# One stage for keys, values and queries: values made transposed, pieces turned by transposing DMAs

## The chip, the cores and the metric

The kernel runs on one core of a Trainium2 chip. The metric is the device time of one execution in microseconds; the median of three runs of the kernel before is 1968.65 us (1966.84 to 1968.81).

## What is computed

Two layers over x (8 x 256 tokens = 2048, 512 wide) and a context of the same size. The changed part is the first half of the second layer, cross attention with 16 heads of 32 columns, where queries and keys are quantised per row and head, values per column over all tokens:

```python
q = (x @ Wq + bq).reshape(1, B * N, H, hd)
kv = (cond @ Wkv + bkv).reshape(1, -1, 2, H, hd)
k, v = (kv[:, :, 0], kv[:, :, 1])
q = jnp.transpose(q * scale, (0, 2, 1, 3))
k = jnp.transpose(k, (0, 2, 1, 3))
v = jnp.transpose(v, (0, 2, 1, 3))
q = _fq_sym(q, axis=-1)      # s = max|q| / 127; round(q / s) * s
k = _fq_sym(k, axis=-1)
v = _fq_sym(v, axis=2)       # one scale per head and column
attn = jnp.einsum('bhqd,bhkd->bhqk', q, k)
attn = jax.nn.softmax(attn.astype(jnp.float32), axis=-1)
attn = _fq_unsigned(attn, axis=-1)
out = jnp.einsum('bhqk,bhkd->bhqd', attn, v)
```

Here x is normalised per row first, and cond is the context. Around it stand a first attention, a gated network of 4-bit weights, the projection and a ternary network.

## The kernel before

The stages follow one another in `build` (L117), each a block of its own: `mix_rows`, `gated_ffn`, `keys_values`, `queries`, `attend`, `project`, `ternary_ffn`. A block starts when all engines have left the one before. P is 128, NT = 16 tiles of 128 tokens, CH = 4 chunks of 128 columns.

`keys_values` (L1049) loops over 16 tiles of tokens. SyncE fetches a tile of the transposed context (`cT`, 256 KB, two buffers, L1101). TensorE makes the keys (`psK`, L1207) and the values (`psV`, L1213), each four f32 products of 128x128 by 512 columns, which the trace shows as eight instructions, and then turns the previous tile's key pieces by 16 transposes of 128x128 bf16 (`psT`, L1220). VectorE adds both biases (L1149, L1152), takes each head's maximum (L1155), quantises the keys (L1156 to L1160) and splits them into three bf16 parts, high, middle and low, of which the fourth quarter is zero (L1167 to L1169); ScalarE copies the high part (L1134), takes the values' sizes (L1130) and stores the turned pieces in `KT` (L1122). After the loop the values' scales are made from a running maximum by transposes and products with the identity (L1235, L1239), and VectorE and GpSimd scale all 16 tiles of values (L1115, L1195), which VectorE rounds into `V` (L1198).

`queries` (L1243) loads its weights (L1277), and per tile VectorE normalises x (L1290), TensorE transposes it (`psX`, L1352), ScalarE copies that (L1327), TensorE multiplies (`psQ`, L1359), VectorE adds the bias, quantises and writes three copies (L1297 to L1309), TensorE turns them by 16 transposes (L1366) and ScalarE stores them in `QO` (L1332).

The order on every engine is the order of the program; engines wait for one another by semaphores only. `attend` (L1387) reads `KT`, `QO` and `V`; its first product is at L1454. Its turned probabilities come from a transposing DMA (L1443), and `gated_ffn` uses the same kind for 128 x 2048 bf16 (L808).

## Time and profile before

| | us |
|---|---|
| median of three runs | 1968.65 |
| the profiled execution | 1971.55 |
| its span, first to last instruction | 1969.8 |
| TensorE busy in it | 1760.5 |
| VectorE busy | 1584.5 |
| ScalarE busy | 1230.8 |
| GpSimd busy | 918.7 |

The span is one execution on the hardware profiler's clock, from the first to the last instruction. Busy time counts an engine's own instructions; matmuls are pipelined, so the start of one and the start of the next tell the pace better than the durations. In the timeline a row is a run of like instructions: start, length, engine, line, operation, written tile, read tiles, shapes, count, and in brackets the idle time before it and what ended it. PEclk is TensorE's granted clock as a share of full speed.

### The profile page before, as it was taken

To read this page: it belongs to the slowest core of one execution; us is meant where nothing else is said; L and a number is where in the kernel's file an instruction comes from. 1 tells how busy PE (TensorE), PEld (TensorE's weight loads), DVE (VectorE), ACT (ScalarE), POOL (GpSimd) and SP (SyncE) were. 2 spreads that over 40 slices of the span, in tenths; PEclk is the share of its full clock that TensorE was granted. 3 is DMA by queue.
4 is the path that set the end of the run, shared out by engine and by line. 5 is a ranking of instruction groups with operands and counts; after the bars stand their busy time and mean duration, and the time that the engine had idled before them with its cause. 6 is when DMAs were issued, how large, how long until landed. Compare 5 with 4: busy or idle time off the path is not lost. (4 is left out here: it accounts for less than half of the span.)

```text
span 1969.8 us, 32510 instructions
## 1 busy us (share of the span) xinstructions
PE 1760.5 (89%) x11262; PEld 786.4 (40%) x11262; DVE 1584.5 (80%) x2930; ACT 1230.8 (62%) x2011; POOL 918.7 (47%) x935
## 2 busy tenths in 40 slices
PE   4999989599999969939899999999999969579998
PEld 1322322144444435425344444444444434234443
DVE  5899999776776678868899999999999956774433
ACT  4888876455454324414599999999999965222111
POOL 6576764464544300020188888888888850000000
PEclk8999999799999989959899999999999989799999
DMA  9764640300000021000054555555565553000000
GB/s 210 205 163 108 160 119 12 110 11 11 22 0 22 0 80 34 24 27 0 16 108 108 108 108 107 109 106 110 103 109 108 108 131 142 6 6 17 22 22 22
DMA packets 334720, 147.54 MB, mean 75 GB/s; under 512 B 290544, under 2 KB 306928, under 8 KB 333424
## 3 DMA queue, kind: packets, MB, share of 16 engines
q1 hardware_dynamic: 334576, 145.70, 31.8%
q8 instruction: 81, 1.33, 0.3%
q14 instruction: 63, 0.52, 0.1%
HBM read 70.15 MB, written 4.19 MB: 38 GB/s over the span
## 5 line engine op out<-in xcount | busy, mean ns | idle before, releaser
L1571 ACT ACTIVATE a_prob<-a_psS,a_bias,q_scale 128x1024 uint8<-128x1024 f32 x512 | 610.2, 1211 | 28.3 <-PE a_psS L1464 24.4
L1500 DVE TENSOR_REDUCE a_tops<-a_psM 128x1 f32<-128x512 f32 x1024 | 622.6, 677 | 2.2 <-PE a_psM L1454 0.8
L1550 POOL CAST a_wide<-a_pairs 128x2048 int16<-128x2048 uint8 x256 | 481.4, 1891 | 99.5 <-DMA a_pairs<-a_prob 84.8
L1454 PE MATMUL a_psM<-KT,QO 128*128 128x512 bf16 x1024 | 370.7, 387 | 5.6 <-PEq L1248 2.2
L1464 PE MATMUL a_psS<-KT,QO 128*128 128x512 bf16 x1024 | 305.4, 380 | 4.3 <-ACT a_prob L1571 4.3
L1476 PEld LDWEIGHTS a_psO<-V,a_wide 128*128 128x128 f16 x4096 | 175.1, 96 | 146.4 <-DVE QO L1513 23.0
L1476 PE MATMUL a_psO<-V,a_wide 128*128 128x32 bf16 x4096 | 181.5, 177 | 21.8 <-DVE QO L1513 15.6
L854 DVE SCALAR_TENSOR_TENSOR g_sum<-g_psG,gu_scale,g_sum 128x512 f32<-128x512 f32 x176 | 124.2, 745 | 89.7 <-PE g_psG L1006 74.9
L832 POOL TENSOR_TENSOR g_sum<-g_sum 128x512 f32<-128x512 f32 x88 | 126.3, 1436 | 140.4 <-DVE g_sum L854 140.4
L489 ACT ACTIVATE prob<-psT 128x512 f32<-128x512 f32 x256 | 142.9, 598 | 68.5 <-PE psT L698 68.1
L953 ACT ACTIVATE g_sum<-g_psG,gu_scale 128x512 f32<-128x512 f32 x176 | 111.2, 681 | 109.6 <-PE g_psG L1006 108.9
L554 DVE TENSOR_REDUCE rmax<-psS 128x1 f32<-128x512 f32 x256 | 158.6, 673 | 12.1 <-PE psS L684 10.5
L1019 PE MATMUL g_psY<-raw_dn,g_hT 128*128 128x512 f32 x352 | 163.1, 592 | 0.0
L1454 PEld LDWEIGHTS a_psM<-KT,QO 128*128 128x128 bf16 x1024 | 96.9, 96 | 137.4 <-DVE a_tops L1500 133.3
L1845 ACT ACTIVATE t_h<-t_psH,t_b 128x512 f32<-128x512 f32 x64 | 44.0, 687 | 162.3 <-PE t_psH L1869 143.5
L684 PE MATMUL psS<-ks,qs 128*128 128x512 f16 x256 | 93.1, 395 | 41.9 <-POOL qs L413 22.0
L1464 PEld LDWEIGHTS a_psS<-KT,QO 128*128 128x128 bf16 x1024 | 96.4, 98 | 68.7 <-ACT a_prob L1571 12.6
L413 POOL TENSOR_TENSOR qs<-xs,q_sub 128x512 f16<-128x512 f32 x64 | 74.8, 1191 | 87.6 <-ACT q_sub L481 83.3
L1571 ACT ACTIVATION_READ_ACCUMULATOR a_prob<-a_psS,a_bias,q_scale 128x1 f32 x512 | 105.5, 206 | 0.0
L1869 PE MATMUL t_psH<-t_xT_hi,t_w1q 128*128 128x512 f16 x256 | 98.4, 385 | 6.6 <-ACT t_h L1845 5.1
L1881 PE MATMUL t_psY<-t_w2q,t_hT_hi 128*128 128x512 f16 x256 | 99.1, 387 | 2.0 <-DVE t_hT_lo L1806 2.0
L694 PE MATMUL psT<-qs,ks 128*128 128x512 f16 x256 | 98.4, 384 | 0.9 <-ACT prob L489 0.9
(211 smaller groups left out, 2862.0 us busy)
## 6 DMA issues: line engine op xcount, KB each, us to landing
xs<-in_x SPq DMA_DIRECT2D x64, 256.0 KB, 6.5
cs<-in_ctx SPq DMA_DIRECT2D x64, 256.0 KB, 8.4
KT<-in_w SPq DMA_DIRECT2D x2, 4096.0 KB, 21.1
raw_gu<-in_gu SPq DMA_DIRECT2D x4, 1408.0 KB, 8.4
vs<-in_ctxT SPq DMA_DIRECT2D x16, 256.0 KB, 2.8
k_cT<-in_ctxT SPq DMA_DIRECT2D x16, 256.0 KB, 2.7
a_pairs<-a_prob SPq DMA_TRANSPOSE x256, 2.7
out<-x_sb SPq DMA_DIRECT2D x16, 256.0 KB, 2.0
```

What stands on the lines that cost most here:

```text
L489: act.activation(prob[:, g % RING, :], psT[g % NT3][:, :], ACT.Exp, scale=float(D0) ** -0.5).then_inc(exped, 1)
L554: v.reduce_max(rmax[j % 2][:, n:n + 1], psS[(NG * j + n) % 3][:, :], AX.X).then_inc(maxed, 1)
L832: pool.tensor_tensor(a[:, :], a[:, :], b[:, :], ALU.add).then_inc(totalled, 1)
L854: v.scalar_tensor_tensor(out=acc[:, :], in0=psG[q % CH][:, :], scalar=gu_scale[:, i * FG + p, g:g + 1], in1=acc[:, :], op0=ALU.mult, op1=A ...
L953: act.activation(part_sum[g][i][m % 3][:, :], psG[q % CH][:, :], ACT.Copy, scale=gu_scale[:, i * FG + p, g:g + 1]).then_inc(scaled, 1)
L1019: mm = pe.matmul(psY[k][:, :], hT[t % 2][:, f, k * P:(k + 1) * P], w_dn[:, f, :], start=(f == 0), stop=(f == FG - 1))
L1454: pe.matmul(psM[n % NM][:, :], QOf[:, i * P:(i + 1) * P], KTf[:, keys:keys + 512], start=True, stop=True).then_inc(shown, 1)
L1464: mm = pe.matmul(psS[g % NS][:, c * 512:(c + 1) * 512], QOf[:, i * P:(i + 1) * P], KTf[:, keys + c * 512:keys + (c + 1) * 512], start=True ...
L1476: mm = pe.matmul(psO[:, h * D1:(h + 1) * D1], wide[i % NV][:, parity, c, :].bitcast(F16), V[:, h, 2 * c + parity, :], start=(parity == 0 a ...
L1500: v.reduce_max(tops[i // JOIN % NB][:, i % JOIN, c:c + 1], psM[n % NM][:, :], AX.X).then_inc(topped, 1)
L1550: pool.tensor_copy(wide[i % NV][:, :, :, :].rearrange("p k c q -> p k (c q)"), both).then_inc(widened, 1)
L1571: act.activation(prob[i % NP][:, k * HK:(k + 1) * HK], psS[g % NS][:, :], ACT.Exp, scale=q_scale[:, i:i + 1], bias=bias[i // JOIN % NB][:, ...
```

## The change

`keys_values` and `queries` become one stage, `keys_values_queries`. The values are made transposed, 128 columns by 512 tokens in a unit, with the weights' columns as the stationary operand; ScalarE adds their bias while it empties the bank, and a unit of 128 columns over all 2048 tokens (four units) is quantised at once by VectorE. Products of values and keys alternate in the order of the list `ORDER` over four banks, `psA`, which the queries use too. The biases of keys and queries are added as one more product: rows of three bf16 parts, made by `bias_rows`, with ones. The high and middle parts of the keys are the upper half-words of f32 numbers, copied by ScalarE; VectorE makes the rest and the low part. The pieces of keys and queries and the quantised values are turned by transposing DMAs from SyncE (16 + 16 + 4, 512 KB each) in place of TensorE's transposes and ScalarE's copies. The loops are written out. The weights, the context and the values lie where `QO` will be written. `V` has its dimensions in another order, and tokens lie in it in another order to match the turned probabilities, which `KT`'s interleaving did before.

Removed lines are those of the two functions printed above; from the new function the core is shown.

```diff
@@ -115,7 +115,7 @@
 
 
 def build(nc, x_in, ctx_in, ctxT_in, gamma_in, gu_in, gus_in, dn_in, dns_in, wq_in, bq_in, wkv_in,
-          bkv_in, wp_in, bp_in, w1_in, b1_in, w2_in, b2_in, out):
+          bkv_in, bv_in, wp_in, bp_in, w1_in, b1_in, w2_in, b2_in, out):
     with ExitStack() as ctx:
         def sb(name, shape, dt):
             return ctx.enter_context(nc.sbuf_tensor(name, shape, dt))
@@ -154,12 +154,11 @@
             def asb(name, shape, dt):
                 return att.enter_context(nc.sbuf_tensor(name, shape, dt))
 
-            env["V"] = asb("V", [P, H1, NT, D1], BF16)
+            env["V"] = asb("V", [P, NT, H1, D1], BF16)
             env["v_scale"] = asb("v_scale", [P, CH], F32)
-            keys_values(env, ctxT_in, wkv_in, bkv_in)
             env["QO"] = asb("QO", [P, NT * H1, P], BF16)
             env["q_scale"] = asb("q_scale", [P, NT * H1], F32)
-            queries(env, wq_in, bq_in)
+            keys_values_queries(env, ctxT_in, wkv_in, bkv_in, bv_in, wq_in, bq_in)
             env["e_sum"] = asb("e_sum", [P, NT * H1 * 2], F32)
             attend(env)
             project(env, wp_in, bp_in, w1_in, w2_in)
@@ -1046,11 +1045,13 @@
                     down(*t_f_k)
 
 
-def keys_values(env, ctxT_in, wkv_in, bkv_in):
-
-
-
-    nc, KT, V, v_scale, id_f, id_b = (env[n] for n in ("nc", "KT", "V", "v_scale", "id_f", "id_b"))
+def keys_values_queries(env, ctxT_in, wkv_in, bkv_in, bv_in, wq_in, bq_in):
...
+    nc, x_sb, KT, V, v_scale, QO, q_scale, id_f, mv, rstd = (env[n] for n in (
+        "nc", "x_sb", "KT", "V", "v_scale", "QO", "q_scale", "id_f", "mv", "rstd"))
+    NA = 4
+    AHEAD = 4
+    NU = CH * NTC
     with ExitStack() as ctx:
         def sb(name, shape, dt):
             return ctx.enter_context(nc.sbuf_tensor(name, shape, dt))
@@ -1061,327 +1062,339 @@
...
+        words = flat(QO[:, :, :]).bitcast(F32)
+        wkv = words[:, 0:2 * CH * DM].rearrange("p (c n) -> p c n", c=CH)
+        vT = [words[:, 2 * CH * DM + i * TOK:2 * CH * DM + (i + 1) * TOK] for i in range(2)]
+        cT = words[:, 2 * CH * DM + 2 * TOK:].rearrange("p (c n) -> p c n", c=CH)
...
+        UNITS = [(2 * (u // 8) + u % 2, u % 8 // 2) for u in range(NU)]
+        ORDER = [("v", u) for u in range(AHEAD)]
+        for i in range(NU - AHEAD):
+            ORDER += [("k", i), ("v", AHEAD + i)]
+        ORDER += [("k", t) for t in range(NU - AHEAD, NT)] + [("q", t) for t in range(NT)]
+        SLOT = {item: s for s, item in enumerate(ORDER)}
...
+        def high_half(ap):
...
+            return ap.bitcast(BF16).rearrange("p (h d k) -> p h d k", d=D1, k=2)[:, :, :, 1]
...
+        def free(eng, g):
...
+            if g >= 2:
+                eng.wait_ge(turned[g % 2], 16 * (g // 2))
...
+            def turn_values(c):
+                sp.wait_ge(v_ready, c + 1)
+                out = V[:, :, c * HT:(c + 1) * HT, :].rearrange("p t h d -> p t (h d)").bitcast(I16)
+                sp.dma_start_transpose(out, vq[:, :].bitcast(I16)).then_inc(v_turned, 16)
...
+            def turn_keys(t):
+                sp.wait_ge(high_ready, 2 * t + 2)
+                sp.wait_ge(lo_ready, t + 1)
+                sp.dma_start_transpose(KT[:, :, t * P:(t + 1) * P].bitcast(I16),
+                                       parts[t % 2][:, :, :, :].rearrange("p h k d -> p (h k d)").bitcast(I16)
+                                       ).then_inc(turned[t % 2], 16)
...
+            sp.dma_start(bv[:, :], bv_in).then_inc(loaded[0], 16)
+            fetch_wv(0, 0)
+            fetch_ctx(0, 0)
+            fetch_wv(1, 1)
+            fetch_ctx(1, 2)
+            sp.dma_start(raw[0][:, :], bkv_in[0:DM].partition_broadcast(P)).then_inc(loaded[5], 16)
+            sp.dma_start(raw[1][:, :], bq_in.partition_broadcast(P)).then_inc(loaded[6], 16)
+            sp.dma_start(wkv[:, :, 0:DM], wkv_in[:, 0:DM].rearrange("(c p) n -> p c n", p=P)).then_inc(loaded[7], 16)
+            fetch_ctx(2, 3)
+            fetch_ctx(3, 4)
+            fetch_wv(2, 8)
+            fetch_wv(3, 8)
+            sp.dma_start(wq[:, :, :], wq_in.rearrange("(c p) n -> p c n", p=P)).then_inc(loaded[9], 16)
+            for kind, i in ORDER:
+                if kind == "v" and UNITS[i][1] == NTC - 1:
+                    turn_values(UNITS[i][0])
+                if kind == "k":
+                    turn_keys(i)
+                if kind == "q":
+                    turn_queries(i)
...
+            def values(u):
+                c, n = UNITS[u]
+                if u == 0:
+                    act.wait_ge(loaded[0], 48)
+                act.wait_ge(v_done, u + 1)
+                if c >= 2:
+                    act.wait_ge(v_ready, c - 1)
+                act.activation(vT[c % 2][:, n * TC:(n + 1) * TC], bank("v", u)[:, :], ACT.Identity,
+                               bias=bv[:, c:c + 1]).then_inc(v_out, 1)
...
+                free(act, t)
+                act.activation(parts[b][:, :, 0, :], high_half(khat[:, :]), ACT.Copy).then_inc(high_ready, 1)
+                act.wait_ge(rest_ready, t + 1)
+                act.activation(parts[b][:, :, 1, :], high_half(rest[:, :]), ACT.Copy).then_inc(high_ready, 1)
...
+            def transposed(t):
+                act.wait_ge(x_turned, t + 1)
...
+                act.activation(xT[t % 2][:, :, :], psX[t % 2][:, :, :], ACT.Copy).then_inc(xT_ready, 1)
...
+            def queries(t):
+                p = parts[t % 2]
+                act.wait_ge(row_ready, t + 1)
+                act.activation(p[:, :, 1:3, :], p[:, :, 0, :].unsqueeze(2).to_broadcast((P, H1, 2, D1)),
+                               ACT.Copy).then_inc(copied, 1)
+            act.wait_ge(blank, 3)
+            for kind, i in ORDER:
+                if kind == "v":
+                    values(i)
+                if kind == "k":
+                    keys(i)
+                    if i == NT - 2:
+                        transposed(0)
+                        transposed(1)
+                if kind == "q":
+                    queries(i)
+                    if i + 2 < NT:
+                        transposed(i + 2)
...
+            def bias_rows(i):
+                own = Counter(v, b_own, 5 * i)
+                v.wait_ge(loaded[5 + i], 16)
+                b, r = raw[i], kn
+                high = [by_head(m[:, :]) for m in (b, r)]
+                own.link(v.tensor_tensor(by_head(r[:, :]), high[0], high_half(b[:, :]), ALU.subtract))
+                own.link(v.tensor_tensor(by_head(khat[:, :]), high[1], high_half(r[:, :]), ALU.subtract))
+                own.link(v.tensor_scalar(khat[:, :], khat[:, :], id_f[:, 2:3], None, ALU.mult))
...
+            def values(u):
+                c, n = UNITS[u]
+                v.wait_ge(v_out, u + 1)
+                v.tensor_reduce(v_max[:, c, n:n + 1], vT[c % 2][:, n * TC:(n + 1) * TC], AX.X, ALU.max,
+                                apply_absolute_value=True).then_inc(v_sized, 1)
+                if n == NTC - 1:
+                    quantise(c, u)
...
+            def quantise(c, u):
+                own = Counter(v, v_own, 4 * c)
+                at = slice(c, c + 1)
+                v.wait_ge(v_sized, u + 1)
...
+                own.link(v.tensor_scalar(vT[c % 2], vT[c % 2], v_inv[:, at], ROUND, ALU.mult, ALU.add))
+                if c:
+                    v.wait_ge(v_turned, 16 * c)
+                v.tensor_scalar(vq[:, :].rearrange("p (c k m) -> p c k m", k=2, m=P),
+                                vT[c % 2].rearrange("p (c m k) -> p c k m", k=2, m=P), ROUND, None,
+                                ALU.subtract).then_inc(v_ready, 1)
...
+            def keys(t):
+                own = Counter(v, k_own, 4 * t)
+                source = by_head(bank("k", t)[:, :])
...
+                own.link(v.tensor_reduce(scale[:, :], source, AX.X, ALU.max, apply_absolute_value=True))
...
+                v.tensor_tensor(by_head(kn[:, :]), source, inv[:, :].unsqueeze(2).to_broadcast(heads),
+                                ALU.mult).then_inc(k_read, 1)
+                v.wait_ge(k_read, t + 1)
...
+                if t >= 1:
+                    v.wait_ge(high_ready, 2 * t)
+                v.tensor_tensor(by_head(khat[:, :]), by_head(kn[:, :]), scale[:, :].unsqueeze(2).to_broadcast(heads),
...
+                v.wait_ge(khat_ready, t + 1)
+                v.tensor_tensor(by_head(rest[:, :]), by_head(khat[:, :]), high_half(khat[:, :]),
+                                ALU.subtract).then_inc(rest_ready, 1)
+                v.wait_ge(rest_ready, t + 1)
+                free(v, t)
+                v.tensor_tensor(parts[t % 2][:, :, 2, :], by_head(rest[:, :]), high_half(rest[:, :]),
+                                ALU.subtract).then_inc(lo_ready, 1)
...
+            def normalise(t):
+                if t >= 4:
+                    v.wait_ge(x_turned, t - 1)
+                v.tensor_scalar(xn[t][:, :], x_sb[:, t, :], mv[:, t, 0:1], rstd[:, t:t + 1],
+                                ALU.subtract, ALU.mult).then_inc(xn_ready, 1)
...
+            def queries(t):
+                own = Counter(v, q_own, 3 * t)
+                source = by_head(bank("q", t)[:, :])
+                at = slice(t * H1, (t + 1) * H1)
+                v.wait_ge(q_done, t + 1)
...
+                v.wait_ge(q_read, t + 1)
+                free(v, NT + t)
+                v.tensor_scalar(parts[t % 2][:, :, 0, :], by_head(kn[:, :]), ROUND, ROUND, ALU.add,
+                                ALU.subtract).then_inc(row_ready, 1)
+                v.wait_ge(row_ready, t + 1)
...
+            for kind, i in ORDER:
+                if kind == "v":
+                    values(i)
+                    if i == 1:
+                        bias_rows(0)
+                    if i == 3:
+                        bias_rows(1)
+                        v.wait_ge(b_own, 10)
+                if kind == "k":
+                    if i == NT - 2:
+                        v.wait_ge(v_ready, CH)
+                        normalise(0)
+                        normalise(1)
+                    keys(i)
+                    if i == NT - 1:
+                        v.wait_ge(high_ready, 2 * NT)
+                        v.wait_ge(lo_ready, NT)
+                        normalise(2)
+                        normalise(3)
+                if kind == "q":
+                    queries(i)
+                    if i + 4 < NT:
+                        normalise(i + 4)
...
+            def release(s):
+                if s >= 0:
+                    kind, i = ORDER[s]
+                    pe.wait_ge({"v": v_out, "k": k_read, "q": q_read}[kind], i + 1)
...
+            def values(u):
+                c, n = UNITS[u]
+                if u in NEEDS:
+                    pe.wait_ge(*NEEDS[u])
+                at = slice(DM + c * P, DM + (c + 1) * P)
+                for i in range(CH):
+                    mm = pe.matmul(bank("v", u)[:, :], wkv[:, i, at], cT[:, i, n * TC:(n + 1) * TC],
+                                   start=(i == 0), stop=(i == CH - 1))
...
+            def keys(t):
+                if t == 0:
+                    pe.wait_ge(loaded[7], 16)
+                    pe.wait_ge(b_own, 10)
+                    pe.wait_ge(blank, 1)
...
+            for s, (kind, i) in enumerate(ORDER):
+                release(s - NA)
+                if kind == "v":
+                    values(i)
+                if kind == "k":
+                    keys(i)
+                    if i == NT - 2:
+                        transpose(0)
+                        transpose(1)
+                if kind == "q":
+                    queries(i)
+                    if i + 2 < NT:
+                        transpose(i + 2)
@@ -1474,7 +1487,7 @@
                     pe.wait_ge(widened, i + 1)
                 for c in range(KC):
                     mm = pe.matmul(psO[:, h * D1:(h + 1) * D1], wide[i % NV][:, parity, c, :].bitcast(F16),
-                                   V[:, h, 2 * c + parity, :], start=(parity == 0 and c == 0),
+                                   V[:, 2 * c + parity, h, :], start=(parity == 0 and c == 0),
                                    stop=(parity == 1 and c == KC - 1))
                 if parity:
                     mm.then_inc(weighed, 1)
@@ -1913,6 +1926,7 @@
         "in_bq": rows(f["L1_xattn_bq"]),
         "in_wkv": rows(f["L1_xattn_Wkv"]),
         "in_bkv": rows(f["L1_xattn_bkv"]),
+        "in_bv": rows(f["L1_xattn_bkv"][DM:].reshape(CH, P).T),
         "in_wp": rows(f["L1_xattn_Wp"]),
         "in_bp": rows(f["L1_xattn_bp"]),
         "in_w1": rows(f["L1_ffn_w1"].T),
```

## Rows read from the trace of the kernel before

**Rows 1.** Windows: busy us of PE, PEld, DVE, ACT, POOL; granted clock, DMA share, GB/s.

```profile
707.00:842.00 135.00, 128.91 (x516) 64.67 (x516) 106.37 (x193) 56.03 (x48) 0.00 (x0) 0.97 0.13 39
...
842.00:871.00 29.00, 2.28 (x9) 1.78 (x8) 21.79 (x32) 1.83 (x1) 12.86 (x10) 0.50 0.10 30
...
871.00:963.00 92.00, 82.21 (x448) 46.62 (x449) 66.68 (x144) 39.61 (x33) 0.00 (x0) 0.95 0.01 5
```

**Rows 2.** Timeline of one pass of keys and values, TensorE.

```profile
763.22 3.65 PE L1207 MATMUL k_psK<-k_w,k_cT 128*128 128x512 f32 x8
...
770.14 1.06 PE L1220 MATMUL k_psT<-id_b,k_parts 128*128 128x128 bf16 x16
...
771.03 3.65 PE L1207 MATMUL k_psK<-k_w,k_cT 128*128 128x512 f32 x8
```

**Rows 3.** Timeline of one pass of queries.

```profile
900.98 3.69 PE L1359 MATMUL q_psQ<-q_w,q_xT 128*128 128x512 f32 x8
...
906.08 3.65 PE L1359 MATMUL q_psQ<-q_w,q_xT 128*128 128x512 f32 x8
...
906.28 0.55 DVE L1290 TENSOR_SCALAR q_xn<-x_sb,x_mv,x_rstd 128x512 f32 x1 [0.44 <-DVE q_q L1297]
...
909.57 0.60 PE L1352 MATMUL q_psX<-id_f,q_xn 128*128 128x128 f32 x4
...
910.09 1.07 PE L1366 MATMUL q_psT<-id_b,q_copies 128*128 128x128 bf16 x16
```

**Rows 4.** Timeline between the two loops.

```profile
839.46 1.62 PEld L1220 LDWEIGHTS k_psT<-id_b,k_parts 128*128 128x128 bf16 x16 [5.91 <-DVEq L1170]
...
867.00 0.38 SPq L1277 DMA_DIRECT2D q_w<-in_wq  x1
...
873.65 1.94 PE L1352 MATMUL q_psX<-id_f,q_xn 128*128 128x128 f32 x8 [27.25 <-DVE q_xn L1290]
...
875.42 4.92 PE L1359 MATMUL q_psQ<-q_w,q_xT 128*128 128x512 f32 x7
```

**Rows 5.** Timeline at the start of keys and values.

```profile
701.27 0.38 SPq L1101 DMA_DIRECT2D k_cT<-in_ctxT  x1
...
707.35 5.76 PE L1207 MATMUL k_psK<-k_w,k_cT 128*128 128x512 f32 x8 [16.01 <-DMA k_w<-in_wkv]
...
711.37 0.48 DVE L1175 MEMSET k_vabs<- 128x512 f32 x1 [5.77 <-DMA k_bias<-in_bkv]
...
712.95 3.60 PE L1213 MATMUL k_psV<-k_w,k_cT 128*128 128x512 f32 x8
```

**Rows 6.** Timeline from the last query pieces to attention's first product.

```profile
959.73 0.90 PEld L1366 LDWEIGHTS q_psT<-id_b,q_copies 128*128 128x128 bf16 x16 [3.35 <-DVE q_copies L1309]
...
960.83 1.88 ACT L1332 ACTIVATE QO<-q_psT 128x2048 bf16<-128x2048 bf16 x1 [2.37 <-PE q_psT L1366]
...
963.02 10.41 PE L1454 MATMUL a_psM<-KT,QO 128*128 128x512 bf16 x18 [2.22 <-PEq L1248]
```

**Rows 7.** Timeline of one pass of keys and values, VectorE and ScalarE.

```profile
763.35 0.67 DVE L1155 TENSOR_REDUCE k_scale<-k_k 128x16 f32<-128x512 f32 x1
...
764.55 0.69 DVE L1158 TENSOR_TENSOR k_kn<-k_k,k_inv 128x512 f32<-128x512 f32 x1
...
765.27 0.43 DVE L1159 TENSOR_SCALAR k_kn<-k_kn 128x512 f32<-128x512 f32 x1
...
765.73 0.69 DVE L1160 TENSOR_TENSOR k_khat<-k_kn,k_scale 128x512 f32<-128x512 f32 x1
...
766.54 0.63 ACT L1134 ACTIVATE k_parts<-k_khat 128x512 bf16<-128x512 f32 x1 [2.21 <-DVE k_khat L1160]
```

**Rows 8.** SyncE's timeline, then the DMA view of 590 to 602 (KB, us to landing).

```profile
594.18 2.63 SPq L808 DMA_TRANSPOSE g_xT_lo<-g_half_lo  x1
...
g_xT_hi<-g_half_hi SPq DMA_TRANSPOSE x1, 3.9
g_xT_lo<-g_half_lo SPq DMA_TRANSPOSE x1, 4.3
```

345 lines of the change are left out of this document (86 added, 259 removed).

## The prediction

> **What bounds the kernel now.** I read the page's chain of waits first, and it says nothing of the changed stretch: followed back from the last instruction, it ends long before. So the stretch is priced by its own clock. The windows [rows 1] give it three parts. From 707 to 842 us TensorE is busy 128.91 of 135 us and is the bound; from 842 to 871 it is busy 2.28 of 29; from 871 to 963 it is busy 82.21 of 92. The timeline gives the pace. One pass over 128 tokens of keys and values starts its keys' product at 763.22 and the next at 771.03 [rows 2], a pitch of 7.81 us: two groups of eight f32 instructions (6.92 together) and 16 bf16 transposes (0.89). One pass of queries starts at 900.98, the next at 906.08 [rows 3], 5.1 later. Between the two loops the values are scaled, the queries' stage issues its first load only at 867.00, and TensorE's next product runs at 875.42 [rows 4]. The stretch lasts from 701.27 us, its first issue [rows 5], to 963.02, attention's first product [rows 6]: 261.8 us. What stands before it is untouched; attention, the projection and the last network keep their instructions, and in one operand of attention only the order of the 32-wide runs changes. So the forecast is the new length of this stretch.
>
> **The prices.** TensorE: a pass of an f32 group takes 0.43 (sixteen with their entry 6.92 [rows 2]), a group of eight 3.43, and 5.60 when it starts from rest (707.35 to 712.95 [rows 5]). Sixteen bf16 passes of 128 columns take 0.89 [rows 2], so one of 512 columns some 0.22. Four f32 transposes with their entry are 0.52 (909.57 to 910.09 [rows 3]). VectorE, with some 0.03 between linked instructions: reduction and the two small ones on 16 columns together 1.20 (763.35 to 764.55), tensor by tensor 0.72, rounding 0.46 [rows 7], normalising 0.55 [rows 3]. ScalarE: 512 columns 0.63 [rows 7], 2048 columns 1.88 [rows 6], so 1024 some 1.05. Hand-overs: 0.12 from VectorE to ScalarE (766.42 to 766.54 [rows 7]); I take 0.2 to 0.25 from TensorE to the others and back.
>
> **Steady keys and values.** TensorE per pair: 3.43 for a value unit (128 channels by 512 tokens, again eight instructions) and 3.43 + 0.22 for keys with the bias as a product, 7.08 in all; the 16 transposes go to a DMA. VectorE per pair: 1.20 + 0.72 + 0.46 + 0.73 + 0.69 = 3.80 up to the rest. Then a new wait: ScalarE, in its order, copies the rest's high half (0.12 + 0.63), only then empties the value unit (0.05 + 0.63), and VectorE's maximum over that unit stands behind it (0.17 + 0.70). The pair is 3.80 + 2.30 = 6.10, under 7.08, so TensorE still bounds. The low half (0.69) lies inside that wait. POOL keeps only its fills. SP gains 36 turning DMAs of 512 KB. The trace has the same size: the second of two issued back to back, at 594.18, held SP for 2.63 and landed after 4.3, the first after 3.9 [rows 8]. Whatever one costs in bandwidth is under that, against 7.08 per pair. A buffer of pieces is wanted again two pairs later, so the landing is hidden.
>
> **The start.** The first unit needs 1.25 MB, as the first product did before (256 KB and 1 MB), plus one issue of 0.5 and a tiny transfer: start 708.0 for 707.35 [rows 5]. The first four units end at 708.0 + 5.60 + 3 x 3.43 = 723.9. Now the keys wait for both bias rows. VectorE's order puts row 0 behind the second maximum and row 1 behind the fourth. Each is five full-width instructions, four with two tensors at 0.72 and one at 0.50: 3.4. The fourth maximum ends at 723.9 + 0.25 + 0.63 + 0.17 + 0.70 = 725.7, the row at 729.1, so TensorE stands still for 5.3 us. Is it cold then? After 5.9 idle the 16 weight loads of the transposes took 1.62 us [rows 4], after 3.35 idle 0.90 [rows 6]: yes, so I charge the cold entry again, 5.60 - 3.43 = 2.2. Its lower bound is 0. First keys done: 729.2 + 3.65 + 2.2 = 735.05. One unit and eleven pairs follow: 735.05 + 3.43 + 77.9 = 816.4 for the last value unit, 809.3 for the one before.
>
> **The hand-over.** A chunk of 128 channels is quantised when its fourth unit is there: three small ones (0.6), a 2048-column multiply-add, and a rounding to bf16 that reads every second word. At the rate of the 512-column row (0.43, of which some 0.16 is fixed) the first takes 1.3. The second has no row: 1.26 at that rate, 2.3 at the rate of the two-tensor rows (0.69 for 512 [rows 7]). I take 2.3, as no row reads every second word. So 4.2 a chunk. The Trainium skill (VectorE: DVE Perf Modes, Mode 2×_2P — use both read ports for one tensor) lets a one-source f32 instruction in SBUF use both ports without asking for neighbouring elements, which would make it 1.26 and the sum 2 us lower; no row here shows that mode with a stride. The first two chunks end in the middle, and their 8.4 us fit: TensorE has four banks and wants a keys' bank 10.5 us after filling it, normally read after 2.1, and VectorE regains 1 us a pair. The last two chunks end right before four keys without values, where TensorE makes one in 3.65 and VectorE takes 4.6. VectorE: maximum of unit 14 done 812.4, chunk 816.6, keys 11 821.2, unit 15 822.7, chunk 826.9, keys 12 and 13 836.1, two normalised tiles 837.2, keys 14 841.8. TensorE is through keys 14 at 827.3 and waits until 836.8 for the first normalised tile: 9.5 us idle. It turns two tiles cold (1.8 before the product of 875.42 [rows 4]), makes keys 15 until 843.7 and the first query product until 847.4, waits for normalised tile 2 (849.3), and the second product ends at 853.6. The third needs a tile that ScalarE copies behind the first query's pieces: 849.9 + 2.35 + 0.12 + 1.05 + 0.65 + 0.2 = 854.3.
>
> **Queries and the end.** TensorE per tile: 3.49 + 0.22 + 0.52 = 4.2. The loop from the end of product t to the start of product t+2 is 0.4 + 2.4 on VectorE (1.20 + 0.72 + 0.43), 0.12 + 1.05 for the two copies, 0.65 for the next transposed tile and 0.23 back, 4.8; with 3.7 for a product two tiles take 8.5, so the pitch is 4.25 instead of 5.1. The last product starts at 854.3 + 13 x 4.25 = 909.6 and ends 913.3, VectorE 915.9, ScalarE 917.0. Only here does a turning DMA lie open: 0.1 + 3.9, and 0.5 for the end of the block, 921.5. Before, TensorE and one copy of 1.88 stood there [rows 6]. The stretch is 220.2 instead of 261.8, 41.5 us less (963.0 - 921.5). The profiled execution lasted 1971.55 with a span of 1969.8, so a like execution would last 1930.0; the median of the runs is 1968.65, 2.9 lower, and 41.5 off that gives 1927.
>
> **The rivals.** First, VectorE and ScalarE bound the pairs. For it: two of VectorE's instructions and both copies of ScalarE read every second half-word, of which no row shows the price, and ScalarE's order is interleaved. Against it: 6.10 against 7.08, and one half-word in four bytes is the traffic of f32. At 8.1 a pair, 12 pairs cost 12 us and the six keys at the hand-over 6: 1945. Second, the idle spots are smaller: no cold entry at 729 and 837 (3.7), rounding at the fast rate (2): 1921. Third, the slower one: the turning DMAs bound the queries. Two buffers leave a DMA 2 x 4.25 - 1.6 = 6.9 us from the copies to the next write into that buffer, against 3.9 in the trace. Beyond 6.9 each us L of landing costs 8 in the loop's 16 tiles and 1 at the end: 8 x (L - 6.9) + (L - 3.9). At 8 us that is 13, so 1940; it eats the gain at 11.2, and at 12 the time is 1976. Only the shape speaks for it: the destination in KT is 256-byte runs 4 KB apart. Fourth, the change does not do what it says because loads starve it. The third unit wants 2.5 MB by 715, the keys 4 MB by 724; before, 2.75 MB were there by 711.4 [rows 5]. With 10 us of stall 1937.
>
> **How the numbers follow.** Forecast 0.70 at 1927; VectorE and ScalarE as bound 0.10; smaller idle spots 0.08; starving loads 0.05; DMA-bound queries 0.07, of which 0.04 slower. The range takes in the second case and reaches to the first: from 1914 (all low ends, and a hand-over shorter by another 7) to 1944 (two waits of 0.2 more per query tile, 6.4, a landing of 5.6, 1.7, and 9 from pairs slower than 7.08). About 0.2% (4 us) is what a measurement of this kernel can tell from no change: faster 0.92, same 0.03, slower 0.05.
>
> **What would show it.** A pair's pitch of 7.08 with TensorE full; about 5 us idle before the first keys and 9 to 10 before the first transposed query tile; queries' pitch 4.2 to 4.3; turning DMAs landing in about 4; attention's first product near 922. A pair over 7.1 with TensorE waiting for VectorE or ScalarE shows the first rival, waits for the pieces' DMA the third, waits for loads the fourth. If attention changes its own length, the premise is wrong.

## The result and the profile after

The changed kernel takes 1920.86 us (median of 4 runs, 1919.58 to 1925.15) against 1968.62 (4 runs, 1966.84 to 1968.81): a ratio of 0.9763 with a 95% interval of 0.9746 to 0.978. The forecast was 1927, so the sign and the range held, and the gain is 47.8 us instead of 41.5. The profiled execution took 1919.65 with a span of 1917.7.

Of the 52.1 us between the two spans 4.2 lie ahead of the changed stretch, in code that is the same in both (its first issue is at 697.08 for 701.27; over all profiles of this study it lies between 695.9 and 706.0, whatever was edited). From attention's first product to the end it is 1006.7 after and 1006.8 before, so the premise that attention keeps its length held. From its first issue to its first product the stretch takes between 6.0 and 7.1 us in the changed kernel and its variants, so differences of half a microsecond between their stretches say little. The stretch itself went from 261.75 to 213.9, so 47.8 us lie in it. By its parts, from the first and last products in the timelines:

| part of the stretch | before | after | difference |
|---|---|---|---|
| first issue to first product | 6.1 | 6.6 | +0.5 |
| keys' and values' products, up to the end of the last | 125.3 | 132.0 | +6.7 |
| from there to the first query product | 42.75 | 0 | -42.75 |
| query products | 80.1 | 66.75 | -13.3 |
| last query product to attention's first product | 7.5 | 8.5 | +1.0 |

The 132.0 us after hold more than products: the stall before the first keys, and the whole hand-over to the queries with its idle time, since the last keys are made behind the first transposed query tiles. So the third row went to 0 partly by moving into the second.

Windows of the changed kernel (columns as in [rows 1]: window, its length, busy us and count of PE, PEld, DVE, ACT, POOL, granted clock, DMA share, GB/s). The windows are the start, the steady pairs, the hand-over and the queries:

```profile
701.00:735.00 34.00, 26.13 (x52) 11.33 (x54) 13.96 (x25) 4.05 (x7) 0.00 (x0) 0.85 0.59 212
735.00:810.00 75.00, 74.84 (x179) 33.27 (x181) 59.15 (x107) 18.91 (x31) 0.00 (x0) 1.00 0.49 91
810.00:860.00 50.00, 42.43 (x116) 20.26 (x117) 40.04 (x80) 14.02 (x21) 0.00 (x0) 0.93 0.61 112
860.00:920.00 60.00, 51.30 (x144) 21.72 (x145) 38.12 (x81) 18.82 (x23) 0.43 (x2) 0.88 0.60 108
```

The second window is a TensorE that never rests, with a granted clock of 1.00 (2.4 GHz). The row of [rows 1] in which TensorE was busy 2.28 of 29 us has no counterpart: the emptiest windows now are the start, 26.13 of 34, and the hand-over, 42.43 of 50. The start, timeline of the changed kernel:

```profile
697.08 0.36 SPq L1153 DMA_DIRECT2D k_bv<-in_bv  x1
...
703.69 15.96 PE L1353 MATMUL k_psA<-QO 128*128 128x512 f32 x32 [16.55 <-DMA QO<-in_ctxT]
...
724.77 5.35 PE L1364 MATMUL k_psA<-QO 128*128 128x512 f32 x8 [5.12 <-DVE k_bias_q L1243]
...
730.17 3.60 PE L1353 MATMUL k_psA<-QO 128*128 128x512 f32 x8
```

Keys 0 wait 5.12 us for the second bias row, and then take 5.35 where the next group takes 3.60: the granted clock is 0.51 from 724.7 to 728.2, after 1.00 from 708 to 719. The two, 5.12 and 1.75, are the price of the start, 6.9 us. A pair in the middle:

```profile
740.68 3.60 PE L1364 MATMUL k_psA<-QO 128*128 128x512 f32 x8
...
744.53 0.69 DVE L1272 TENSOR_REDUCE k_scale<-k_psA 128x16 f32<-128x512 f32 x1 [1.30 <-PE k_psA L1365]
...
747.77 3.60 PE L1364 MATMUL k_psA<-QO 128*128 128x512 f32 x8
...
748.39 0.63 ACT L1201 ACTIVATE k_parts<-k_rest 128x512 bf16<-128x512 bf16 x1
...
748.93 0.67 ACT L1192 ACTIVATE QO<-k_psA,k_bv 128x512 f32<-128x512 f32 x1
...
749.63 0.69 DVE L1249 TENSOR_REDUCE k_v_max<-QO 128x1 f32<-128x512 f32 x1 [0.55 <-ACT QO L1192]
...
750.93 1.29 DVE L1261 TENSOR_SCALAR QO<-QO,k_v_inv 128x2048 f32<-128x2048 f32 x1
...
752.25 1.23 DVE L1264 TENSOR_SCALAR k_vq<-QO 128x2048 bf16<-128x2048 f32 x1
```

From 740.68 to 747.77 is 7.09, against 7.81 in [rows 2]. VectorE waits for TensorE (1.30) before its pass, which runs from 744.53 to 750.32, 5.8 us. A ScalarE copy that reads every second half-word takes 0.63, as one that reads f32 does [rows 7]. The hand-over:

```profile
827.84 1.00 DVE L1294 TENSOR_SCALAR QO<-x_sb,x_mv,x_rstd 128x512 f32<-128x512 f32 x2
...
828.43 1.97 PE L1372 MATMUL k_psX<-id_f,QO 128*128 128x128 f32 x8 [5.82 <-DVE QO L1294]
...
835.72 3.60 PE L1381 MATMUL k_psA<-k_wq,k_vq 128*128 128x512 f32 x8
...
835.92 0.69 DVE L1272 TENSOR_REDUCE k_scale<-k_psA 128x16 f32<-128x512 f32 x1 [2.63 <-PE k_psA L1365]
...
841.18 0.66 PE L1372 MATMUL k_psX<-id_f,k_khat 128*128 128x128 f32 x4 [1.65 <-DVE k_khat L1294]
```

TensorE waits 5.82 us for the first two normalised tiles, where it waited 27.25 before [rows 4]. Then it makes keys 15 at a granted clock of 0.50 (828.4 to 833), and now VectorE waits, 2.63 us, for these keys. Last, two query products in a row and the end:

```profile
866.21 3.60 PE L1381 MATMUL k_psA<-k_wq,k_vq 128*128 128x512 f32 x8
...
869.35 0.58 ACT L1209 ACTIVATE k_vq<-k_psX 128x512 f32<-128x512 f32 x1
...
870.30 3.60 PE L1381 MATMUL k_psA<-k_wq,k_vq 128*128 128x512 f32 x8
...
902.26 0.38 PE L1382 MATMUL k_psA<-k_bias_q,k_ones 128*128 128x512 bf16 x1
...
905.16 1.06 ACT L1214 ACTIVATE k_parts<-k_parts 128x1024 bf16<-128x1024 bf16 x1 [2.94 <-DVE k_parts L1310]
...
911.01 10.42 PE L1467 MATMUL a_psM<-KT,QO 128*128 128x512 bf16 x18 [8.37 <-PEq L1055]
```

A tile of queries takes 4.09 instead of the 5.1 of [rows 3]. Behind the last product lie VectorE's pass, one copy, and then 4.8 us (906.22 to 911.01) in which the last turning DMA lands and the block ends. The DMA view (name, count, us to landing) of 701 to 918:

```profile
V<-k_vq SPq DMA_TRANSPOSE x4, 4.2
...
QO<-k_parts SPq DMA_TRANSPOSE x16, 4.2
```

### The profile page after: what moved, and what is told of

It reads as the page before. It is cut to its first block and busy times, and to the rows that moved or that the text cites. A ratio compares the mean times of both kernels' runs of the same rounds, so it can differ in the third digit from the quotient of the medians.

```text
span 1917.7 us, 30705 instructions
## 1 busy us (share of the span) xinstructions
PE 1715.1 (89%) x10617; PEld 758.6 (40%) x10770; DVE 1527.1 (80%) x2832; ACT 1190.2 (62%) x2011; POOL 909.1 (47%) x926
## 5 line engine op out<-in xcount | busy, mean ns | idle before, releaser
L1467 PE MATMUL a_psM<-KT,QO 128*128 128x512 bf16 x969 | 353.9, 387 | 21.8 <-DVE a_tops L1513 10.4
L1477 PE MATMUL a_psS<-KT,QO 128*128 128x512 bf16 x966 | 292.7, 380 | 6.7 <-ACT a_prob L1584 3.7
L1550 POOL TENSOR_TENSOR a_low<-a_top,a_less 128x2 f32<-128x2 f32 x128 | 25.1, 196 | 223.4 <-DVE a_top L1521 223.4
```

The costliest lines, as they stand in the source:

```text
L1467: pe.matmul(psM[n % NM][:, :], QOf[:, i * P:(i + 1) * P], KTf[:, keys:keys + 512], start=True, stop=True).then_inc(shown, 1)
L1477: mm = pe.matmul(psS[g % NS][:, c * 512:(c + 1) * 512], QOf[:, i * P:(i + 1) * P], KTf[:, keys + c * 512:keys + (c + 1) * 512], start=True ...
```

## The experiments

The first four are edits of the changed kernel, run on one chip with the kernel before (1968.68).

**e1_rows_early: take the stall away.** In VectorE's program, both bias rows go ahead of everything that needs a product:

```diff
             normaliser(v, env)
+            bias_rows(0)
+            bias_rows(1)
+            v.wait_ge(b_own, 10)
             for kind, i in ORDER:
                 if kind == "v":
                     values(i)
-                    if i == 1:
-                        bias_rows(0)
-                    if i == 3:
-                        bias_rows(1)
-                        v.wait_ge(b_own, 10)
```

> The changed kernel with both bias rows made before the first maximum instead of behind the second and the fourth; nothing else differs. Theory: the rows are what TensorE waits for before the first keys (5.12 us idle there, and a cold entry of 5.35 - 3.43 = 1.9 behind it), and TensorE bounds what follows, so the stretch gets 7.0 us shorter and attention starts 7 us sooner: 1914. Rival A: the keys' weights are the next thing late; they were issued at 700.89 and took 11.4, so they land at 712.3, before the 719.5 at which the keys would start, and this should cost nothing; if it does, the idle stays. Rival B: the 7 us are given back at the hand-over to the queries, where VectorE is last: then 1919 to 1921 and a longer idle spot before the first transposed query tile.

Measured: 1912.4 us, a ratio of 0.9718 (0.9701 to 0.9734); the stretch is 207.0, 6.9 shorter, of which 0.4 is an earlier first product. Its timeline, TensorE around keys 0:

```profile
722.59 3.60 PE L1362 MATMUL k_psA<-QO 128*128 128x512 f32 x8
726.02 0.38 PE L1363 MATMUL k_psA<-k_bias_k,k_ones 128*128 128x512 bf16 x1
```

No idle time, and a group at the full rate. So both the wait and the cold entry were the rows', and neither was given back later.

**e2_pe_turns: put the work of the transposes back on TensorE.** After each keys' and each query product sixteen transposes of the identity into a bank that nobody reads; everything else stays.

```diff
+            def turn16():
+                for h in range(H1):
+                    pe.transpose(psT[:, h, :], id_b[:, :], id_b[:, :])
...
                 pe.matmul(out[:, :], ones_b[:, :], rows[0][:, :], start=False, stop=True).then_inc(k_done, 1)
+                turn16()
...
                 pe.matmul(out[:, :], ones_b[:, :], rows[1][:, :], start=False, stop=True).then_inc(q_done, 1)
+                turn16()
```

> The changed kernel with 16 bf16 transposes of 128x128 (of the identity, into a spare bank, read by nobody) added on TensorE behind each keys' and each queries' product: the work on TensorE that the turning DMAs replaced, without its waits. Theory: TensorE bounds the pairs and the queries, so 12 pairs and 16 query tiles grow by 0.89 each, 24.9 us; the four lone keys hide theirs under VectorE: 1946. That would be the worth of taking the transposes from TensorE. Rival (VectorE and ScalarE bound both loops): nothing in the pairs, nothing in the queries, 1921 to 1925.

Measured: 1935.65 us, 0.9841 (0.9825 to 0.9858); the stretch is 232.6, 18.6 longer, where 24.9 were expected. The pairs paid in full: first keys to last value unit grew by 11.4, 12 times 0.95. The queries grew by 11.4 too, less than the 14 expected, mainly because the wait of 1.65 us between their first two products went and the last set lies behind the last product. The hand-over got 3.7 shorter although it holds four more sets of transposes: TensorE came to it later and waited 1.11 us instead of 5.82. The start was 0.5 shorter. Two query products of this kernel:

```profile
880.41 1.06 PE L1351 MATMUL k_psT<-id_b 128*128 128x128 bf16 x16
...
881.74 3.60 PE L1388 MATMUL k_psA<-k_wq,k_vq 128*128 128x512 f32 x8
...
886.73 3.60 PE L1388 MATMUL k_psA<-k_wq,k_vq 128*128 128x512 f32 x8
```

The pitch is 4.99 for 4.09. TensorE bounds both loops of the changed kernel: inside them the transposes taken off it are worth their whole time. Over the stretch the 32 sets, 28.5 us of work, are worth 18.6.

**e3_turn_twice: double the turning DMAs.** Each of the first eight tiles of keys and of queries is turned twice; the extra copy goes where a later tile's pieces will overwrite it.

```diff
+            def again(m, t):
+                if t < NT // 2:
+                    sp.dma_start_transpose(m, parts[t % 2][:, :, :, :].rearrange("p h k d -> p (h k d)").bitcast(I16)
+                                           ).then_inc(turned[t % 2], 16)
...
+                u = (t + NT // 2) % NT
+                again(KT[:, :, u * P:(u + 1) * P].bitcast(I16), t)
```

> The changed kernel with every turning DMA of the first eight tiles of keys and of queries issued twice, the extra one into the place of a tile that is turned later; the buffers of pieces wait for both. Theory: the DMA engines have room; the pair of turns lands after 5 to 7 us, under the 6.9 us that two buffers leave, so 0 to 2 us more: 1921 to 1923. Rival (a turn holds the DMA engines for its 4.2 us of landing): two take 8.4, the first eight pairs grow by 1.3 and the first eight query tiles by 4.3, 45 us: 1966.

Measured: 1925.32 us, 0.9786 (0.977 to 0.9802); the stretch is 221.9, 8.0 longer: more than the 0 to 2 of the theory, far from the 45 of the rival. The pairs did not notice it, at a DMA share of 0.96; the query products from the fifth on did:

```profile
858.17 3.67 PE L1391 MATMUL k_psA<-k_wq,k_vq 128*128 128x512 f32 x8 [0.62 <-ACT k_vq L1219]
858.58 2.37 SPq L1141 DMA_TRANSPOSE QO<-k_parts  x1
...
860.99 2.46 SPq L1160 DMA_TRANSPOSE QO<-k_parts  x1
...
861.03 0.43 DVE L1320 TENSOR_SCALAR k_parts<-k_kn 128x512 bf16<-128x512 f32 x1 [1.97 <-DMA QO<-k_parts]
...
863.18 3.67 PE L1391 MATMUL k_psA<-k_wq,k_vq 128*128 128x512 f32 x8 [0.68 <-ACT k_vq L1219]
```

The pitch becomes 5.0, VectorE waits for the DMA (1.97), and SyncE issues one after the other, each in 2.4 to 2.5. So turning DMAs that follow one another take some 2.45 us each, less than the 4.2 to 4.8 of their landing: 512 KB in 2.45 us are some 214 GB/s, and the DMA view shows 212 to 220 GB/s in most slices from 855 to 876. With one per tile that is 60% of the 4.09. The DMA share of the changed kernel over its steady query products (861.9 to 902.8) reads 0.72, which would be 2.9 us each; why the two differ stays open. The slower pitch makes 3.8 of the 8 us. The rest, some 4.4, is one place: the issue at 873.40 takes 3.63 us, TensorE waits 2.36 and then makes a product in 5.37 instead of 3.60 (879.81). Why that issue took longer is not shown.

**e4_norm_early: the first two query tiles are normalised and turned two keys earlier.** In all three engines' programs the place goes from NT - 2 to NT - 4.

```diff
-                    if i == NT - 2:
+                    if i == NT - 4:
                         transpose(0)
                         transpose(1)
```

> The changed kernel with the first two tiles of x normalised before keys 12 instead of before keys 14, and transposed and copied behind keys 12. Theory: VectorE is the bound of the hand-over (four keys at 4.6, two quantised chunks, two normalised tiles, all of which it still does), so TensorE's idle 5.8 us before the first transposed tile goes, but the third query product can only start when VectorE is through keys 15, tile 2 and the first query: 0 to 3 us less, 1918 to 1921. Rival (TensorE's idle spot and the cold passes behind it are themselves the cost): 5.8 + 2 us less, 1913.

Measured: 1919.98 us, 0.976 (0.9744 to 0.9777); the stretch is 214.4, 0.5 longer, so nothing was gained. The idle time moved and stayed:

```profile
818.86 1.23 PE L1372 MATMUL k_psX<-id_f,QO 128*128 128x128 f32 x8 [4.31 <-DVE QO L1294]
...
825.35 0.69 DVE L1272 TENSOR_REDUCE k_scale<-k_psA 128x16 f32<-128x512 f32 x1 [1.63 <-PE k_psA L1365]
...
839.53 0.66 PE L1372 MATMUL k_psX<-id_f,k_khat 128*128 128x128 f32 x4 [3.27 <-DVE k_khat L1294]
```

The wait before the first transposes is 4.31 for 5.82, but VectorE now waits 1.63 for keys that TensorE makes later, and TensorE 3.27 at the end. From the last two chunks on VectorE has more to do than TensorE, but it also waits for products that TensorE makes late and cold: these keys take 5.21 (819.88) instead of 3.60.

The next four ran on one chip, the kernel before at 1966.87. Two are edits of the kernel before.

**e5_before_wq: load the queries' weights while keys and values run.** The weights and the bias row get memory of their own and are issued at the end of the keys' stage.

```diff
             in_pairs(sp, fetch, 2, NT)
+            sp.dma_start(env["q_w"][:, :, :], wq_in.rearrange("(c p) n -> p c n", p=P)).then_inc(env["q_w_in"], 16)
+            sp.dma_start(env["q_bias"][:, :], bq_in.partition_broadcast(P)).then_inc(env["q_w_in"], 16)
```

> The kernel before with one thing changed: the queries' weights and bias are loaded at the end of the keys' loop, into memory that attention and the projection use later, and not at the start of their own stage. Theory: the wait of 6.2 us between 866.7 and 872.9 is the load alone, so 6 us less: 1962.5. This is the part of the gain that one stage for all three has by itself. Rival: the wait is the hand-over of the engines from one block to the next, and nothing is gained.

Measured: 1963.53 us, 0.9982 (0.9973 to 0.9992); the stretch is 5.1 shorter, where 6 were expected, and the median 3.3. What is late next is GpSimd, which still fills the stage's buffers with zeros:

```profile
866.09 1.00 DVE L1294 TENSOR_SCALAR q_xn<-x_sb,x_mv,x_rstd 128x512 f32<-128x512 f32 x2 [1.39 <-POOL q_copies L1287]
```

**e6_before_no_tail: the kernel before without the scaling of the values at its end.** It leaves out the maximum over all tokens and the scaling by it: values are rounded as they are, inside the pass.

```diff
-                v.tensor_tensor(vabs[:, :], size[b][:, :], vabs[:, :], ALU.max).then_inc(abs_ready, 1)
+                v.tensor_scalar(V[:, :, bass.ds(t, 1), :], vt.rearrange("p (h a d) -> p h a d", a=1, d=D1),
+                                ROUND, ROUND, ALU.add, ALU.subtract).then_inc(abs_ready, 1)
```

> The kernel before without the values' tail: each tile of values is rounded unscaled inside the loop, in the place of the running maximum, and the scale is set to 1; the maximum over all tokens, its transposes and products and the scaling of the 16 tiles are left out, so the values are not the reference's. Theory: the tail from 842.2 to 867.0 us goes whole, since TensorE bounds the loop and nothing runs beside the tail: 24.5 us less, 1944. Rival: the loop pays part of it back, because VectorE's rounding and the store hold the next tile: 1950 or more.

Measured: 1943.29 us, 0.988 (0.9864 to 0.9897); the stretch is 23.25 shorter, in the profile of the longest of its five runs; the median is 23.6 lower. Of the gap of 42.75, some 23 are this tail and some 5 the load; for the remaining 14 (42.75 less the two, from two separate kernels) the draining of one stage and the filling of the next are left, which no run took apart.

**e8_ahead2: e1 with two value units instead of four ahead of the keys.**

```diff
-    AHEAD = 4
+    AHEAD = 2
```

The query tiles are normalised and turned at NT - 2, as in the changed kernel.

> The changed kernel with the bias rows first, the first two tiles of x normalised and transposed behind keys 14, and two value units ahead instead of four, so that two lone keys stand before the queries and not four. Against the run with the rows alone moved (1912.4). Theory: VectorE is last in the hand-over, and what it has to do from the first of the two last chunks on is two keys less; counted through, it is done 2 us earlier: 1910. Rival A: the lone keys themselves are the cost, at 4.6 - 3.65 each, and the cold TensorE, 5 us less: 1907. Rival B: the keys now ask for their weights 15.6 us after the first issue, the time at which they landed (15.2), and wait for them: 1913 or more.

Measured: 1913.23 us, 0.9732 (0.9716 to 0.9749); the stretch is 206.9 for e1's 207.0, where 2 us less were expected. The sum hides two parts. The keys now come two units earlier, and they wait:

```profile
713.95 0.75 DVE L1243 SCALAR_TENSOR_TENSOR k_bias_q<-k_vq,id_f,k_khat 128x512 bf16<-128x512 bf16 x1
...
714.80 3.67 PE L1362 MATMUL k_psA<-QO 128*128 128x512 f32 x8 [2.69 <-issue]
```

They start 0.1 us behind the second bias row. So the start is 2.6 longer than e1's for the same products, and what follows, less two units of 3.43, is 2.6 shorter: the gain in the hand-over came, and the start took it back.

**e9_pool_low: e1 and e4, and the keys' low part on GpSimd.** GpSimd is idle in this stretch; it takes the last 0.69 us of each pass. VectorE waits for the low part before it writes the next rest, and one normalisation goes ahead of its wait for the last low part.

```diff
-                free(v, t)
-                v.tensor_tensor(parts[t % 2][:, :, 2, :], by_head(rest[:, :]), high_half(rest[:, :]),
-                                ALU.subtract).then_inc(lo_ready, 1)
...
+            for t in range(NT):
+                pool.wait_ge(rest_ready, t + 1)
+                free(pool, t)
+                pool.tensor_tensor(parts[t % 2][:, :, 2, :], by_head(rest[:, :]), high_half(rest[:, :]),
+                                   ALU.subtract).then_inc(lo_ready, 1)
```

> The changed kernel with the bias rows first, the first two tiles of x normalised before keys 12, and the keys' low part made by GpSimd instead of VectorE. Against the run with the rows alone moved (1912.4). Theory: VectorE bounds the hand-over, so each keys' tile there is 0.7 us shorter: five or six tiles, 4 us less, 1908.5; in the pairs TensorE bounds and nothing changes. Rival A: GpSimd's instruction (1.3 us for one of this size before) slows VectorE's beside it, as at 849 to 858 us in the trace of before, where a rounding took 1.4 instead of 0.4, and the gain is lost or turned round: 1912 to 1918. Rival B: VectorE was not the bound, TensorE's idle spot has another cause: 1912.

Measured: 1912.88 us, 0.9727 (0.9711 to 0.9744); the stretch is 207.6, 0.6 longer than e1's. Its hand-over:

```profile
813.61 1.97 PE L1374 MATMUL k_psX<-id_f,QO 128*128 128x128 f32 x8 [4.45 <-DVE QO L1298]
...
820.64 0.69 DVE L1277 TENSOR_REDUCE k_scale<-k_psA 128x16 f32<-128x512 f32 x1 [2.89 <-PE k_psA L1367]
...
824.54 1.04 POOL L1185 TENSOR_TENSOR k_parts<-k_rest 128x512 bf16<-128x512 f32 x1 [5.67 <-DVE k_rest L1291]
...
825.22 0.39 DVE L1278 TENSOR_SCALAR k_scale<-k_scale 128x16 f32<-128x16 f32 x1
```

GpSimd does it in 1.04, but the order of e4 makes VectorE wait 2.89 us, the engine that this was to relieve: TensorE turned two tiles cold and only then made the keys that VectorE wanted. That is a theory of the order, and the last three runs test it (one chip, the kernel before at 1966.44).

**e13_order, e11_pool_order, e12_pool_order_ahead2.** e13 is e1 with a mended order: VectorE normalises the two tiles before keys 12 (NT - 4), TensorE turns them only behind keys 13 (NT - 3), so that a keys' product always lies ready for VectorE. In VectorE's program, and then in TensorE's (ScalarE's changes in the same way):

```diff
-                    if i == NT - 2:
+                    if i == NT - 4:
                         v.wait_ge(v_ready, CH)
                         normalise(0)
                         normalise(1)
...
-                    if i == NT - 2:
+                    if i == NT - 3:
                         transpose(0)
                         transpose(1)
```

e11 is e13 with the low part on GpSimd (the diff of e9). e12 is e11 with AHEAD = 2 (the diff of e8), the tiles normalised before keys 14 and turned behind keys 15.

> The changed kernel with the bias rows first, two tiles of x normalised before keys 12 and transposed and copied behind keys 13, where VectorE has them ready in time. Against the run with the rows alone moved (stretch from first issue to attention 207.0 us). In the earlier placement behind keys 12 TensorE waited 4.3 us for the tiles and VectorE then 1.6 to 2.9 us for cold keys 13. Theory: VectorE, never idle between unit 14 and the third query product, is the bound, so the idle spot goes and the end hardly moves: stretch 205 to 207, 1911. Rival: TensorE's idle and cold time was the cost: 5 to 7 less, 201.

> As the run before in this call, and the keys' low part made by GpSimd. Theory (VectorE bounds the hand-over): its lone keys take 4.08 to 4.3 instead of 4.6 to 4.9, five of them, and no TensorE idle spot hides it this time: 2.5 to 3.5 us less than the same without GpSimd. Rival (something else holds the third query product, such as ScalarE's order): within 0.5 us of it.

> As the second run of this call, with two value units ahead instead of four, the two tiles of x normalised before keys 14 and transposed behind keys 15. Theory: two more us less than with four ahead, since VectorE's idle microsecond of two more pairs is used before the last chunks: stretch 201 to 202, 1906. Rival: the start pays for it by waiting for the keys' weights, 0 or more.

| kernel | median us | ratio to before (95%) | stretch |
|---|---|---|---|
| changed kernel | 1920.86 | 0.9763 (0.9746 to 0.978) | 213.9 |
| e1_rows_early | 1912.4 | 0.9718 (0.9701 to 0.9734) | 207.0 |
| e13_order | 1912.0 | 0.9722 (0.9706 to 0.9738) | 206.8 |
| e11_pool_order | 1909.01 | 0.9708 (0.9692 to 0.9724) | 203.8 |
| e12_pool_order_ahead2 | 1911.99 | 0.9726 (0.971 to 0.9742) | 206.7 |

e13 alone gains nothing over e1, e11 gains 3.0 of stretch over e13. Yet in e13 VectorE has no wait left up to the third query tile:

```profile
830.87 0.55 DVE L1294 TENSOR_SCALAR k_khat<-x_sb,x_mv,x_rstd 128x512 f32<-128x512 f32 x1
...
831.47 1.12 PE L1370 MATMUL k_psX<-id_f,k_khat 128*128 128x128 f32 x4 [5.18 <-DVE k_khat L1294]
832.38 6.07 PE L1379 MATMUL k_psA<-k_wq,k_vq 128*128 128x512 f32 x8
```

Counted from the first issue, VectorE has normalised this tile after 134.1 us, 3.1 sooner than in e1. TensorE gives it back: it stands 5.18 us before the tile, and then turns it in 1.12 instead of 0.66 and makes the second query product in 6.07 instead of 3.60 (granted clock 0.57 from 831.4 to 838.3; in e1 the idle time there is 1.65 and the clock 1.00). The timeline of e11:

```profile
810.57 1.11 PE L1374 MATMUL k_psX<-id_f,QO 128*128 128x128 f32 x8 [0.80 <-DVE QO L1298]
...
814.02 0.69 DVE L1291 TENSOR_TENSOR k_rest<-k_khat 128x512 f32<-128x512 f32 x1
...
818.09 0.69 DVE L1291 TENSOR_TENSOR k_rest<-k_khat 128x512 f32<-128x512 f32 x1
...
828.38 1.12 PE L1374 MATMUL k_psX<-id_f,k_khat 128*128 128x128 f32 x4 [4.43 <-DVE k_khat L1298]
```

VectorE makes one keys after the other without a wait, 4.07 us each, and the idle spot ahead of the first transposes is 0.80 us; 4.43 stand at the second spot. The tile there is normalised 1.6 us sooner than in e13, and the product behind it takes 4.65 for 6.07; together they are the 3.0. e11 is the fastest kernel of the study. By the ratios, each against the kernel before on its own chip, it takes 0.9708 / 0.9763 = 0.9944 of the changed kernel's time, and the two intervals do not touch.

e12 fell: 2.9 longer than e11, where a gain of 2 was expected. Its start:

```profile
707.83 0.69 DVE L1242 TENSOR_TENSOR k_kn<-k_rest 128x512 f32<-128x512 f32 x1 [6.52 <-DMA k_rest<-in_bkv]
...
714.13 0.75 DVE L1248 SCALAR_TENSOR_TENSOR k_bias_q<-k_vq,id_f,k_khat 128x512 bf16<-128x512 bf16 x1
...
714.99 1.53 PE L1366 MATMUL k_psA<-QO 128*128 128x512 f32 x3 [3.24 <-issue]
```

The row to be split lands at 707.8, VectorE needs 7.1 us for both, and the keys, which now come two units earlier, start at 715.0 behind 3.24 us of idle: the stall of the changed kernel is back at another size, as in e8. It makes the start 3.4 longer than e11's for the same products; only 0.5 comes back behind it. The profile names only "issue"; the keys start 0.1 us after the second row's end.

## Why the prediction was right, and where it was off

**The large terms.** What the stretch lost is what was forecast: the transposes off TensorE, and the gap between the loops filled. The pair's pitch came out at 7.08 to 7.09 (forecast 7.08), the start to first keys at 27.7 (27.9), the pairs to the last value unit at 86.7 (87.2). The stall was 5.12 (5.3) and the cold entry 1.75 (2.2); e1 showed both. e2 showed that the pairs were TensorE's by the whole price.

**The hand-over was mis-sized, 3.1 us of the 6.3 by which the stretch is shorter than forecast.** The step that failed is "I take 2.3, as no row reads every second word". The rounding of 2048 columns took 1.23. A chunk is 3.1 us, not 4.2, so VectorE is earlier by 2.2 after the last two, and a pass of keys takes it 4.47 where the sum had 4.6, so 0.4 over three. What is left of the 3.1 is spread over waits that I did not take apart. The Trainium skill (VectorE: DVE Perf Modes, Mode 2×_2P — use both read ports for one tensor) let this instruction use both ports in spite of its stride. The trace agrees: 1.23 for the one with the stride, 1.29 for the one without. I had put the rule beside the sum and taken the other end, by the rate of two-tensor rows; the nearest row was that of the one-tensor instruction of 0.43. TensorE waited 5.82 and 1.65 us instead of 9.5 and 1.9. What sets the length of the hand-over is shown in part. VectorE's work is in it: 0.69 off each pass brought 3.0 (e11 against e13). But it is not VectorE's sum alone: in the changed kernel VectorE itself waits 2.63 us for cold keys, and where an order took such a wait away (e13: -0.2) TensorE's cold product took its place.

**The queries' pitch was mis-sized, 2.85 us.** The step is "the loop ... 4.8; with 3.7 for a product two tiles take 8.5". The prediction had this loop through VectorE and ScalarE as the bound and TensorE, at 4.2, just under it; it is the other way round. The loop is shorter: in the changed kernel's timeline it is some 4.2 us from the end of one product to the release of the next but one, so two tiles need 7.9 by it. The pitch of 4.09 is TensorE's own sum, 3.43 + 0.22 + 0.44 (866.21 to 870.30). My 4.2 had added the entry of a group to the product and to the transposes as if each paid it. Over thirteen tiles the 0.16 is 2.1 us; the rest came from shorter waits of the first three tiles. e2 confirms the bound: 0.90 more per tile for 0.89 more work.

**The end**, 8.5 for 8.2, was 0.3 too low: the last DMA landed in 4.2, not 3.9.

**The rivals.** The first (VectorE and ScalarE bound the pairs) did not come: reading every second half-word costs 0.63 on ScalarE and 0.69 on VectorE, as f32 does. The second (smaller idle spots) held by half: rounding at the fast rate, yes; no cold entry, no. The third (turning DMAs bound the queries) did not come, and its condition was not near. The buffers leave 2 x 4.09 - 1.6 = 6.6 us for a landing of 4.2, so by the prediction's own sum they would bind at a tile of 2.9 us (an estimate). e3 adds a second condition, that the DMAs follow one another no faster than every 2.45 us. The fourth (loads starve it) did not come: the first four units run on without a gap, and e8 and e12 showed that what early keys wait for are bias rows. The measured median is the 1921 of the second rival, but that is a coincidence: one of its two terms came, and the queries' pitch, which it did not have, made up the rest.

The median gained 47.8, 6.3 more than forecast, as much as the stretch is shorter than forecast. The 4.2 us of the profiled execution ahead of the stretch are not of the change.

## What to carry to other kernels

Price a new instruction by the row of its own kind (one tensor or two), not by the one that looks most like its operand; where a known instruction and a new one differ only in a stride, keep both ends and take the nearer kind. When the gap between two stages is filled, follow both engines through the filling: here work taken off VectorE shortened it, and an order that spared VectorE a wait was worth nothing while it left TensorE a long idle spot, whose price is paid again in the slow product behind it. When a stretch does not change, look at its parts: in e8 a gain and a loss of 2.6 us cancelled. And look at the first use of every small operand: 7 us here were two rows of 512 numbers that nobody had to make so late.

## What the runs showed of the hardware

- A transposing DMA of 512 KB within SBUF has two prices: it lands after 4.2 us alone, and one that follows another comes 2.45 us after it (e3). At the end of the chain the first one shows; in e3's loop the second set the pitch.
- While GpSimd works on its two-tensor instruction of 1.04, VectorE's 16-column instruction beside it takes 0.39 instead of 0.17 (e9 and e11, line 1278) and ends 0.03 us behind GpSimd's (815.86 and 815.83 in e11); the 512-column reduction ahead of it, which reads PSUM, keeps its 0.69. A pass takes 4.07 instead of 4.47, though an instruction of 0.69 was taken off. In the kernel before, VectorE's 512-column product of two SBUF operands takes 1.79 beside GpSimd's (847.27) and 0.68 once GpSimd is done (859.67).
- After 4.31 us of idle time the eight transposes took 1.23 (e4), after 4.45 us 1.97 (e9), after 5.82 us 1.97 in the changed kernel. In e4 the slow part only came later: the granted clock was 1.00 from 818.8 to 819.6, then 0.50 from 819.8 to 822, and the keys behind took 5.21 instead of 3.60. What TensorE had done before differs between them, so no length of idle time is read from this.
